# Graph attention in a four-layer GNN kernel: rows gathered per edge tile, maxima by segmented scans, and weighted one-hots in the second pass

## The reference

```
h = node_features @ W
s_src = h @ a[:d_out]
s_tgt = h @ a[d_out:]
e = leaky_relu(s_src[src] + s_tgt[tgt], 0.2)
m = segment_max(e, tgt)
e_exp = exp(e - m[tgt])
denom = segment_sum(e_exp, tgt)
attention = e_exp / denom[tgt]
h_prime = segment_sum(h[src] * attention[:, None], tgt)
return elu(h_prime)
```

## Time and profile before

| | |
|---|---|
| median of three runs | 16392.38 us |
| the profiled execution's own time | 16381.74 us |
| its span | 16379.9 us |
| PE, DVE, ACT, POOL busy | 53%, 44%, 14%, 57% |
| mean granted TensorE clock | 0.662 of 2.4 GHz |

### The profile page before, as it was taken

How to read it: one execution, slowest core, us unless ns; L and a number is a source line. 1 busy time by engine, 2 the same in 40 slices (tenths; PEclk the granted TensorE clock), 3 DMA queues, 4 the chain that set the end, 5 groups by cost and what they waited for, 6 DMA issues and landing times.

```text
span 16379.9 us, 185197 instructions
## 1 busy us (share of the span) xinstructions
PE 8638.3 (53%) x50470; PEld 7567.5 (46%) x50471; DVE 7134.3 (44%) x11630; ACT 2338.6 (14%) x3624; POOL 9283.4 (57%) x8334
## 2 busy tenths in 40 slices
PE   4777777745555556885544445995222223222223
PEld 4777777744555545775444445884111112111112
DVE  5444444434444446995333334555233233333333
ACT  0111111111212114662000001332000001000000
POOL 2888888836666663002666664001766665666774
PEclk7666666667666667997677766665555556555556
DMA  4333333323333333331211111111111111111111
GB/s 80 18 18 18 18 18 18 18 64 103 99 102 102 102 100 100 99 99 46 46 45 45 45 45 46 49 49 44 35 34 34 34 34 38 34 34 34 34 34 32
DMA packets 858162, 838.25 MB, mean 51 GB/s; under 512 B 631584, under 2 KB 637940, under 8 KB 855541
## 3 DMA queue, kind: packets, MB, share of 16 engines
q0 software_dynamic: 455488, 397.95, 16.2%
q1 hardware_dynamic: 402639, 439.86, 8.3%
HBM read 580.70 MB, written 256.41 MB: 51 GB/s over the span
## 4 chain that ended last, share of the span: by engine, by line
another core or an unknown queue 22%; issue 22%; PE 21%; DVE 13%; POOL 9%; DMA 7%; DVEq 4%; SPq 2%; ACT 0%; POOLq 0%; ACTq 0%
POOL lane_tab L623 9%; PE ps L1000 6%; DMA lane_tab<-rows,idx 6%; DVE buf_d L1621 3%; PE ps L974 2%; PE ps L975 2%; DVE tmp_c L1478 2%; DVE buf_a L1472 1%; DVE mx L1484 1%; DVE buf_a L410 1%; DVEq L1472 1%; PE ps L1012 1%; PE ps L1040 1%; PE ps L1016 1%
## 5 line engine op out<-in xcount | busy, mean ns | idle before, releaser
L623 POOL DMA_INDIRECT lane_tab<-rows,idx x1664 | 2595.5, 1560 | 790.7 <-issue 789.2
L637 POOL DMA_INDIRECT buf_b<-gcn_tab,idx x1664 | 1654.4, 994 | 2100.2 <-issue 1882.4
L637 POOL DMA_INDIRECT aux<-att_tab,idx x1664 | 1578.9, 949 | 2178.9 <-DVEq L1467 1276.7
L1012 PE MATMUL ps<-ident_b,zero_b 128*128 128x512 bf16 x1664 | 747.4, 601 | 3726.9 <-DVE buf_a L410 2171.8
L1621 DVE TENSOR_REDUCE buf_d<-ps 128x512 f32<-128x1536 f32 x416 | 731.2, 1758 | 3215.2 <-remote 2478.3
L637 POOL DMA_INDIRECT buf_c<-gcn_tab,idx x1664 | 1675.7, 1007 | 726.6 <-issue 509.4
L1012 PEld LDWEIGHTS ps<-ident_b,zero_b 128*128 128x128 bf16 x1664 | 199.1, 133 | 4028.9 <-issue 2606.2
L1073 PE MATMUL ps<-ident,buf_a 128*128 128x128 f32 x3328 | 907.6, 360 | 1102.8 <-issue 860.3
L637 POOL DMA_INDIRECT buf_b<-src_tab,idx x832 | 892.1, 1072 | 673.8 <-issue 255.7
L1073 PEld LDWEIGHTS ps<-ident,buf_a 128*128 128x128 f32 x3328 | 734.3, 269 | 1082.5 <-issue 862.2
L720 ACT ACTIVATE idx<-src_s 128x8 int32 x832 | 173.3, 208 | 7160.1 <-DMA aux<-att_tab,idx 2449.7
(11 more groups left out here) (242 smaller groups left out, 18257.6 us busy)
## 6 DMA issues: line engine op xcount, KB each, us to landing
y_stash<-buf_c SPq DMA_DIRECT2D x208, 512.0 KB
tab<-y_stash SPq DMA_DIRECT2D x208, 512.0 KB, 3.3
h_stash<-aux SPq DMA_DIRECT2D x208, 264.0 KB
aux<-in_edge_attr_dram SPq DMA_DIRECT2D x1696, 32.0 KB
rows<-h_stash SPq DMA_DIRECT2D x104, 264.0 KB, 2.8
tab<-h_stash SPq DMA_DIRECT2D x104, 264.0 KB, 2.7
lane_tab<-rows,idx POOLq DMA_INDIRECT x1664
aux<-att_tab,idx POOLq DMA_INDIRECT x1664
```

The source lines that it names most:

```text
L623: pool.indirect_dma_start(lane_tab[k][:, :], bass.IndirectOffsetOnAxis(ap=idx[:, b, u:u + 1], axis=0), rows[:, b, u, 0:D1], None, compute_ ...
L637: pool.indirect_dma_start(to[q][:, u, :], None, table[:, :], bass.IndirectOffsetOnAxis(ap=idx[:, q, u:u + 1], axis=0)).then_inc(rows_in[q] ...
L1012: pe.matmul(ps[:, 4 * (q % 2) + c, :].rearrange("p (k f) -> p k f", f=P), zero_b[:, :], bc(ident_b[:, :].unsqueeze(1), [P, 4, P]), start=T ...
```

## The change

The two passes of the attention are written anew.

- **Gathers per tile.** The source columns by tile are kept at the start (13 PE transposes and one ACT copy into `src_tiles`) and moved to `gate_s` after layer 0. The first pass gathers TT x 4 x 8 = 1568 tiles instead of 1664 steps. A ring slot is free when its copy to `h_stash` has landed; PE and DVE have no work per group there. ACT also copies each tile's score column to `s_tab`. `h_stash` is now laid out partition, tile, 66.
- **Targets.** A prefix sum of the node degrees gives each node's first edge. POOL scatters s_tgt of every node there (98 indirect DMAs of 128 single floats to `t_first_tab`, zero-filled at the start), ahead of the gathers. They are read back in rows of S edges, and a segmented scan spreads them.
- **Maxima.** After the last gather, 13 PE transposes turn the scores to rows of 1664 edges; DVE runs segmented max scans forwards and backwards, each twice because segments cross rows (the carry goes through PE), and makes all exponents' arguments; ACT takes one exponential over 128x1664. The weights go to `weight_tab`, and 13 POOL gathers and 13 transposes bring them to steps (`weight_s`).
- **Second pass.** DVE makes the one-hot and multiplies it by the weight in one instruction a step; PE has the clearing matmuls and the eight f32 matmuls a group, with two register loads (`rel_s`, and `rel2_s`, which now holds the tile's place in the group's load). SP loads the tiles of a group from `h_stash` at a tile number from a register.

```diff
+def gathers(table, to, idx_ready, free, turns=TURNS, stored=None):
...
+    if stored is None: pool.wait_ge(free, i * RING + (q + 1))
+    else:              pool.wait_ge(stored[q], i * 16 + 16)
...
+pool.wait_ge(s.tpos_clean, 16)
+pool.wait_ge(s.t_places, 1)
+for c in range(CHUNKS):
+    pool.wait_ge(s.node_evacuated, 2 * CHUNKS + c + 3)
+    for w in range(c * WPC, (c + 1) * WPC):
+        pool.indirect_dma_start(t_first_tab[:, :], bass.IndirectOffsetOnAxis(ap=first_i[:, w:w + 1], axis=0),
+                                sums[:, w, 0:1], None).then_inc(s.t_stored, 16)
 pool.wait_ge(s.tab_stored, 2 * CHUNKS * 16)
-gathers(att_tab, att_rows, s.l2_indices, s.l2_rows_used)
+gathers(att_tab, att_rows, s.l2_indices, None, TT, h_stored)
+pool.wait_ge(s.weights_stored, 16)
+for b in range(TB):
+    pool.indirect_dma_start(weight_t[:, b, :], None, weight_tab.rearrange("p (b e) -> (p b) e", e=P), ...)
```

```diff
 # SP
-with sp.Fori(0, TURNS) as i:                      # stash, then wait for the store and for l2_scores
...
+sp.wait_ge(s.t_stored, W * 16)
+sp.dma_start(t_first, t_first_tab[0:P * S, :].rearrange("(p e) a -> p (e a)", e=S)).then_inc(s.t_loaded, 16)
+with sp.Fori(0, TT) as i:
+    for q in range(RING):
+        rows_landed(sp, i, q, 1)
+        sp.dma_start(h_stash[:, bass.ds(i * (RING * G) + q * G, G), :]..., att_rows[q]...).then_inc(h_stored[q], 16)
...
+sp.wait_ge(s.l2_weights, 1)
+sp.dma_start(weight_tab[:, :], weight_e).then_inc(s.weights_stored, 16)
+with sp.Fori(0, TURNS - 1) as i:
+    for q in range(RING):
+        sp.wait_ge(s.l2b_sums, g + (RING + 1))
+        load_h(g + RING, q)
```

```diff
 # DVE, after the last gather
+dve.wait_ge(s.s_turned, 1)
+link(dve.tensor_tensor(score, ps_flat[:, 0:S], hide, ALU.add))
+link(dve.tensor_tensor_scan(upto, cut_at[:, 0:S], score, -BIG, ALU.add, ALU.max))
+link(dve.tensor_tensor_scan(back[:, ::-1], ..., score[:, ::-1], -BIG, ALU.add, ALU.max))
+... carry over PE, two scans of 128, four small ops ...
+link(dve.tensor_tensor_scan(upto, cut_at[:, 0:S], score, carry[:, 4:5], ALU.add, ALU.max))
+link(dve.tensor_tensor_scan(back[:, ::-1], ..., score[:, ::-1], carry[:, 5:6], ALU.add, ALU.max))
+... six elementwise ops of 1664 columns ...
+def weighted_hot(g, q):
+    dve.wait_ge(s.l2b_sums, g + 1)
+    for u in range(G):
+        last = dve.tensor_scalar(l2b_hot[q][:, u, :], iota[:, :], step_col(dst_s, g, u), step_col(weight_s, g, u),
+                                 ALU.is_equal, ALU.mult)
+    last.then_inc(s.l2b_hot, 1)
+weighted_hot(0, 0)
+with dve.Fori(0, TURNS) as i:
+    for q in range(RING):
+        weighted_hot(g + 1, (q + 1) % RING)
+        w0 = load1(mybir.EngineType.DVE, win_s, g, W - 1)
+        dve.wait_ge(s.l2b_sums, g + (RING + 1))
+        dve.wait_ge(s.l2b_added, g + 2)
+        dve.tensor_tensor(a, a, regions(4 + 2 * (q % 2), D1), ALU.add).then_inc(s.l2b_added, 1)
```

More of the change, by code:

```diff
@@ L399, in load8, with load7 @@
                 table[:, bass.ds(g * G, G)], engines=(engine,), min_val=0, max_val=top,
+                skip_runtime_bounds_check_because="the table's entries are clamped to it")
+            return v
+        def load7(engine, table, g, top):
+            _, v = nc.values_load_multi_w_load_instructions(
+                table[:, bass.ds(g * G + 1, G - 1)], engines=(engine,), min_val=0, max_val=top,
                 skip_runtime_bounds_check_because="the table's entries are clamped to it")
@@ L871, in _ @@
                 last.then_inc(s.select_done, 1)
+            pe.wait_ge(s.steps_made, CHUNKS_S)
+            for b in range(TB):
+                last = pe.transpose(region(b, P), src_f[:, b, :], ident[:, :])
+            last.then_inc(s.src_turned, 1)
             pe.sem_inc(s.node_products, 2)
@@ L1060, in _, with to_rows @@
                 lb_products(2 * ITER + k, k, 0, 2 * ITER + k)
+            pe.wait_ge(s.deg_ready, 1)
+            pe.matmul(ps[:, 0, 0:W], below[:, :], deg[:, :], start=True, stop=True)
+            pe.matmul(ps[:, 1, 0:W], ones[:, :], deg[:, :], start=True, stop=True).then_inc(s.deg_summed, 1)
             pe.wait_ge(s.node_in, 5)
             node_product(2 * CHUNKS, wt[0:D, TA:TA + D2], D2, 4)
+            def to_rows(n, cols):
+                pe.wait_ge(s.carry_cols, n)
+                for k, col in cols:
+                    last = pe.matmul(region(k, P), bc(col, [P, P]), ident[:, :], start=True, stop=True)
+                last.then_inc(s.carry_rows, 1)
@@ new lines, in _ @@
+            to_rows(1, [(16, carry[:, 0:1])])
+            to_rows(2, [(20, t_edge[:, S - 1:S])])
+            pe.wait_ge(s.l2_indices, RING * (TT + 1))
+            pe.wait_ge(s.keys_clean, 2)
+            by_block = s_tab.rearrange("p (q b) -> p b q", b=TB)
+            for b in range(TB):
+                last = pe.transpose(region(b, P), by_block[:, b, :], ident[:, :])
+            last.then_inc(s.s_turned, 1)
+            to_rows(3, [(24, upto[:, S - 1:S]), (28, carry[:, 1:2])])
+            pe.wait_ge(s.weights_in, TB * 16)
@@ L1106, in _ @@
-            for b in range(2):
-                l2b_transposes(b, b)
-            for b in range(2):
-                l2b_targets(b, b)
-            with pe.Fori(0, ITER // 2 - 1) as i:
-                for half in range(2):
-                    l2b_turn(i * 2 + half, half)
-            l2b_turn(ITER - 2, 0)
-            for b in range(2):
-                l2b_sums(2 * ITER - 2 + b, 1, b)
+                    bank = 4 + 2 * (q % 2)
+                    pe.wait_ge(s.l2b_added, g + 1)
+                    for c in range(2):
+                        pe.matmul(ps[:, bank + c, :].rearrange("p (k f) -> p k f", f=P)[:, :, 0:D1], zero_b[:, :],
+                                  bc(ident_b[:, 0:D1].unsqueeze(1), [P, 4, D1]), start=True, stop=False, skip_group_check=True)
@@ new lines, in _ @@
+                    rel = load8(mybir.EngineType.PE, rel_s, g, (G - 1) * P)
+                    at = load7(mybir.EngineType.PE, rel2_s, g, (G - 1) * D2)
+                    pe.wait_ge(s.l2b_hot, g + 1)
+                    pe.wait_ge(h_in[q], i * 16 + 16)
+                    for u in range(G):
+                        right = l2b_rows[q][:, 0:D1] if u == 0 else l2b_rows[q][:, bass.ds(at[u - 1], D1)]
+                        last = pe.matmul(ps_flat[:, bass.ds(rel[u] + bank * 512, D1)], l2b_hot[q][:, u, :], right,
+                                         start=False, stop=True, skip_group_check=True)
@@ L1557, in _ @@
[L1557 to L1565 removed]
+            link(dve.memset(dst_e, -1))
```

374 lines of the change are left out of this document (173 added, 201 removed).

## The result

The changed kernel took 15927.72 us (median of 4 runs, 15925.66 to 15930.48) against 16393.43 us (4 runs, 16377.90 to 16414.86): ratio 0.9715, 95% interval 0.9698 to 0.9732. It is 466 us faster where 800 were forecast, and lies 208 us above the range.

What follows compares the result with a forecast made beforehand. POOL's gathers, with 400 us of late slot releases, bound the first pass; PE was busy 1044 of the second's 1157 us. Passes ending 801 us earlier, 1 more behind, gave 16381.7 - 800 = 15581, stated as 15585; range 15440 to 15720.

Steps and rivals of the forecast that it cites:

- the pace of the gathers: First pass: 1568 gathers at 1.251 us take 1962 us, ending at 9638, some 455 us earlier.
- what released POOL late is gone: First pass: a slot needs only its landing and store, so POOL's 400 us of waits vanish.
- answer late: Old first pass: PE and DVE release slots in pairs and late, costing POOL 400 us of its 2484.
- the register loads fit beneath: Second pass: PE's register loads hide under the matmuls, leaving 3.74 us a group, 778 us.
- The rival of the exposed loads: Second pass: PE's queue can't run ahead past waits; 5.2 us a group, 1082 us, total 15885; chance 0.08.
- gaps ahead of L1158: Second pass: PE showing gaps ahead of this line would mean the forecast is wrong.
- The serial part: Between last gather and second pass, engines work one at a time: 63 us, ends 55 and 85.
- The start: Step tables and degrees ahead of the scatters: 2 us and 3 us more, first scatter near 7553.
- POOL sets the pace: Scatters: target chunks come faster than seven scatters, so 98 at 1.25 us take 122 us.
- The high clock: Rival, second pass: clock stays high, DVE's 3.1 us a group bounds, 645 us, total 15450; chance 0.13.
- The late ring: Rival, first pass: store landings still delay POOL's slots, 377 us, total 15960; chance 0.04.
- The serial pass: Rival, second pass: one-hots, sums and additions run one after another, 10 us a group, total 16883; chance 0.03.

Runs made afterwards that it cites:

- c4: Kernel before, unchanged, on a chip where before takes 15091.93 us: 15087.03 us.
- e5: Changed kernel plus 26 unread PE identity transposes ahead of PE's wait for the first pass's gathers: 14755.02 us (before 15087.45 there).
- e15: Changed kernel with PE's second load of eight values, plus a POOL fill of 1300 columns ahead of each eight gathers: 15959.63 us (before 16383.10).
- e7: Changed kernel with PE's second load of eight values, without 192 of 196 stash stores: 15760.05 us (before 16312.51).
- e8: Changed kernel with PE's second load of eight values, without the 98 target scatters: 15662.32 us (before 16312.51).
- e11: Changed kernel with PE's second load of eight values, without one of POOL's two dummy semaphore increments per first-pass group: 15848.52 us (before 16377.64).
- e12: Changed kernel, second load of eight, without one POOL dummy increment and ACT's source-score copy per first-pass group: 15857.81 us (before 16377.64).
- e6: Changed kernel with PE's second register load taking eight values instead of seven, the first unused: 15842.16 us, ratio 0.9670.
- c1: Changed kernel, unchanged, run again with a trace beside the kernel before (16383.58 us): 15921.04 us, ratio 0.9718.
- e16: Changed kernel with PE's second load of eight values, timed once more: 15825.08 us, ratio 0.9653 (before 16383.10).
- e1: Changed kernel without 192 of the 196 stash stores of the first pass: 14744.37 us (before 15087.45 there).
- e3: Changed kernel without the 98 target scatters and SP's wait for them: 14692.01 us (before 15087.45 there).
- e4: Changed kernel without PE's second register load, row blocks read at fixed places: 14672.50 us (before 15087.45 there).

## Why the prediction was wrong

The order of the work, the engine that bounds each stage and the clock were right; the sum failed in two steps, and two smaller terms were off as well. By the marks of the profiled executions (second kind: c4 and e5, on two chips), in us:

| term | forecast | first kind | second kind |
|---|---|---|---|
| first gather, later than before | 65 | 94 | 25 |
| gathers: before's less the changed kernel's | 2481 - 1962 = 519 | 2481 - 2174 = 307 | 2087 - 1963 = 124 |
| from there to the end of the second pass | 1190 - 841 = 349 | 1190 - 946 = 244 | 1175 - 938 = 237 |
| behind the passes, longer by | 1 | 6 | 4 |
| faster by | 802 | 451 | 332 |

**The step that failed most** is the pace of the gathers: "1568 x 1.251 = 1962 us", with "what released POOL late is gone" and its 400 us behind it. The waits did go, but the pace did not stay at 1.25. On the first kind of chip gathers go no faster than one in 1.40 us for long. That is a rate and not a stall (e15), it is there without stores, without scatters and with fewer small instructions (e7, e8, e11, e12), and at first something hides it: 188 gathers at 0.15 us each, a backlog of some 28 us. With the ring out of the way the gathers met that rate: 1568 x 1.40 = 2195, less 28, and 7 for the long gathers at the start, makes 2174, which is what was measured. So 212 us of the missing 351 are this term.

The reading behind it was wrong too. The earlier trace rows name SP's release of a slot as what ended POOL's waits, and it was. That PE and DVE "answer late" because they release in pairs was argued and not seen: on the second kind of chip the same pairs and the same ring never make POOL wait (c4), and on the first SP itself waited mostly for something that the profile does not show (1770.0 us with the releaser "remote", against 95.8 for PE).

The pitch of 1.247 us in the earlier trace rows was real, but it held for sixteen gathers ahead of a pause. The trace of before had a sign that it does not last. In its layer 3, also 128 rows a gather, POOL fetched (before, then c4):

```profile
11500.00:13500.00 2000.00, 490.95 (x2064) 268.56 (x2064) 617.87 (x518) 36.24 (x174) 1396.92 (x1393) 0.57 0.16 34
10660.00:12660.00 2000.00, 602.41 (x2304) 311.75 (x2304) 690.43 (x578) 39.99 (x192) 1531.37 (x1539) 0.56 0.18 38
```

That is one gather in 1.44 us against 1.30, and nowhere in before's three gather stages do 200 gathers in a row come closer than 1.398 us. Named waits (DVE, L1619) again stand in that stretch, 181 us of them, and in c4's they are all but gone (2 us).

**The second step**: "the register loads fit beneath". Exposed were 0.42 us a group, 88 us. The evidence in the earlier trace rows was for loads of eight values, and it holds for them (e6). The change's second load is of seven, from an odd place; no row had its price. The rival of the exposed loads had the right place and the wrong mechanism: not a queue that can't run ahead, but one load of 1.711 us. The forecast's own sign of being wrong, gaps ahead of L1158, came.

**The serial part**: 79.6 us against 63, within its upper end of 85. Seven are the scans. The Trainium skill ("DVE: opcode table, instruction layouts, handler registers and perf-mode slots", section 6) says half throughput; the trace agrees, 3.62 us against 1.89. I had set it aside for the row of the same shape, which was of another operation. Ten are the gap, which goes when the gathers have no backlog (e15). The estimate with the skill's rule, 69 us, is near the 70 that the second kind and e15 show.

**The start**: 10 us late at the first scatter, not explained, and 20 us in waits for chunks, 5.0 us each after 21 scatters, "DVE sums L1522", of which the second kind shows none: there the 98 scatters took 125.6 us, here 142.4. "POOL sets the pace" was all but right only there (one short wait). A slip of little weight: the forecast adds 3 us to get from its sum of 15581.7 to the median, where its own 10.6 gives 15592.

**The rivals.** The high clock did not come: 0.50 over 866 us of sums, and over 779 us without a gap (e6). The Trainium skill ("TensorE: Matmul & The Clock Gate", The HAM clock gate) says that a busy array releases the slow clock; this stream does not bear that out. The late ring did not come: no wait for `h_stored`. Its time, 15960, came nearest to the measured one, but by chance: its mechanism was absent. No rival had a slower pace of the gathers themselves. The serial pass did not come.

**Open.** What it is in the first kind of chip that serves one gather in 1.40 us, lets small instructions of other engines start only 0.70 or 1.40 us apart, and holds semaphores back. The profile shows no queue or transfer for it, and the transfers' own times don't change at gather 189. Every time on record comes with a span and a clock from the profiler, so whether its recording has a part in it can't be told. The late releases that bring before to 1.49 us a gather there are seen, their cause is open too. Reorganising the gathers to move more rows each was not tried.

## What to carry to other kernels

A wait that names its releaser says who came last, not that the resource would be free without the wait: before counting it as gain, look in the same trace for the fastest long stretch of the same operation, here 200 gathers in layer 3, and take the pace from there. Price an instruction by its exact form, down to the number of values and where they begin; one value more, never used, and an even start took 87 us off the pass. When a time may come from another chip, trace both kernels there before explaining a difference.

## What the runs showed of the hardware

- PE's register load in the changed kernel (medians): eight values from a multiple of eight 0.591 us, seven values from one further 1.711 us.
- On one kind of chip gathers of 128 rows go at 1.25 us for some 190 and then at 1.40 (the changed kernel, c1, e6, e7, e8, e11, e12, e16); on the other at 1.25 to the end (e1, e3, e4, e5). On the first a SyncE loop instruction of 37 ns takes up to 1.40 us while that lasts.
- With POOL held to one gather in 1.46 us or more (e15) the first kind shows none of it in that pass.
- A scatter of 128 single values without accumulation takes POOL 0.961 us and 0.30 between two, against 1.560 for the accumulating one in the earlier trace rows.
- A segmented scan over 1664 columns takes 3.62 us, with its start value read from a tile 3.68.
